# Reordered setup of a fused attention and ternary-MLP kernel, its 24 query transfers issued from three engines

## The reference

```
xn = layernorm(x)
h  = xn + cosformer_attn(rmsnorm(xn) * n1w)        # 16 heads of 16, relu(q), relu(k), cos/sin weights,
                                                    # cumulative sums over the 2048 positions
attention part:  h + gelu((rmsnorm(h) * n2w) @ W1 + b1) @ W2 + b2
ternary part:    r = relu(xn @ (tern(W_fc) * s_fc).T + gate * (xn @ V.T @ F.T @ U.T))
                 (r * r) @ (tern(W_proj) * s_proj).T
out = x + attention part + ternary part
```

## Time and profile before

| | us |
|---|---|
| median of three runs | 618.21 |
| the profiled execution: its time | 617.8 |
| the profiled execution: its span | 616.0 |
| PE busy | 586.7 (95%) |
| DVE busy | 409.2 (66%) |
| ACT busy | 364.4 (59%) |
| POOL busy | 221.4 (36%) |
| PE's first instruction of body(0) starts at | 40.14 |

### The profile page before, as it was taken

The page is one execution under the profiler, slowest core; times in us unless marked ns, Lnnn a source line. Parts: engine busy times, 40 slices in busy tenths (PEclk is TensorE's granted clock), DMA queues, the critical chain, the costliest instruction groups (busy, mean ns, idle before and its releaser), DMA issues.

```text
span 616.0 us, 14491 instructions
## 1 busy us (share of the span) xinstructions
PE 586.7 (95%) x5122; PEld 519.4 (84%) x5122; DVE 409.2 (66%) x776; ACT 364.4 (59%) x654; POOL 221.4 (36%) x251
## 2 busy tenths in 40 slices
PE   7768999999999999999999999999999999999996
PEld 6557888989898898988889898988989888898885
DVE  7899784686647865586746866478655867457532
ACT  6485674557646575557645576465754576455642
POOL 7035413372143612435143721436124351336220
PEclk9879999999999999999999999999999999999999
DMA  7871016400462006600163004610066001620001
GB/s 217 244 186 36 18 48 127 104 1 19 104 103 68 17 0 139 133 0 17 34 140 99 0 17 102 107 64 17 0 139 133 0 17 34 140 65 1 3 0 36
DMA packets 27994, 42.03 MB, mean 68 GB/s; under 512 B 9008, under 2 KB 19904, under 8 KB 27968
## 3 DMA queue, kind: packets, MB, share of 16 engines
q1 hardware_dynamic: 26528, 39.59, 27.7%
q10 hardware_dynamic: 1440, 2.10, 1.3%
HBM read 12.31 MB, written 4.19 MB: 27 GB/s over the span
## 4 chain that ended last, share of the span: by engine, by line
PE 84%; DVE 7%; ACT 4%; issue 2%; ACTq 1%; DMA 1%; DVEq 0%; SPq 0%
PE accum L1241 23%; PE dense L1406 9%; PE dense L1226 8%; PE shared L1264 5%; PE ctx_ps L1289 5%; PE dense L1411 5%; PE dense L1276 4%; PE dense L1134 4%; PE shared L1379 3%; PE shared L1148 3%; PE dense L1138 2%; PE dense L1231 2%; PE ctx_ps L1300 2%; PE upd_ps L1314 2%; PE shared L1358 1%
## 5 line engine op out<-in xcount | busy, mean ns | idle before, releaser
L977 DVE TENSOR_TENSOR wide_lo<-wide,wide_hi 128x512 fp32r<-128x512 f32 x128 | 94.7, 740 | 118.5 <-ACT wide_hi L695 100.1
L985 DVE TENSOR_TENSOR weighted<-shared,cst 128x512 f32<-128x512 f32 x128 | 82.8, 683 | 16.5 <-PE shared L1264 16.5
L692 ACT ACTIVATE wide<-dense,b 128x512 f32<-128x512 f32 x64 | 44.0, 688 | 83.1 <-PE dense L1411 82.7
L1241 PE MATMUL accum<-w_hi,wide_hi 128*128 128x256 f32 x256 | 72.6, 284 | 2.2 <-DVE wide_lo L977 2.2
L534 POOL TENSOR_TENSOR state<-state,added 128x544 f32<-128x544 f32 x32 | 43.8, 1369 | 80.7 <-DVE added L1007 80.4
L1241 PE MATMUL accum<-w_lo,wide_hi 128*128 128x256 f32 x256 | 71.8, 280 | 0.0
L1241 PE MATMUL accum<-w_hi,wide_lo 128*128 128x256 f32 x256 | 71.7, 280 | 0.0
L1241 PE MATMUL accum<-prT,wide_hi 128*128 128x256 f32 x256 | 66.1, 287 | 1.2 <-DVE wide_lo L977 1.2
L500 POOL TENSOR_TENSOR arena<-arena,tab 128x256 f32<-128x256 f32 x64 | 49.5, 802 | 43.7 <-DMA q_stack<-arena 43.7
L1241 PE MATMUL accum<-prT,wide_lo 128*128 128x256 f32 x256 | 64.7, 281 | 0.0
L682 ACT ACTIVATE wide<-dense,scales 128x512 f32<-128x512 f32 x64 | 43.9, 686 | 31.2 <-PE dense L1231 31.2
(11 more groups left out here) (176 smaller groups left out, 1490.5 us busy)
## 6 DMA issues: line engine op xcount, KB each, us to landing
k_stack<-weighted SPq DMA_DIRECT2D x96, 128.0 KB, 2.7
q_stack<-arena SPq DMA_DIRECT2D x184, 64.0 KB, 2.3
xin<-L_attn_x SPq DMA_DIRECT2D x16, 256.0 KB, 2.8
out<-late SPq DMA_DIRECT2D x16, 256.0 KB, 2.2
tab<-trig SPq DMA_DIRECT2D x8, 258.0 KB, 2.7
arena<-L_ffn_w_fc SPq DMA_DIRECT2D x1, 1024.0 KB, 7.4
late<-L_ffn_w_proj SPq DMA_DIRECT2D x1, 1024.0 KB, 7.4
late<-L_attn_mlp_w ACTq DMA_DIRECT2D x1, 1024.0 KB, 5.4
```

The costliest lines, as they stand in the source:

```text
L692: act.activation(wide[:, m % 2, :], dense[m % 2][:, :], ACT.Gelu_apprx_tanh, bias=b1[:, m:m + 1]).then_inc(dense_free, 1)
L977: dve.tensor_tensor(wide_lo[:, n % 2, :], wide[:, n % 2, :], wide_hi[:, n % 2, :].bitcast(F32), ALU.subtract).then_inc(lo_done, 1)
L985: dve.tensor_tensor(weighted[:, g, :].rearrange("p (a n) -> p a n", a=4), shared[g % 2][:, :].rearrange("p (a n) -> p a n", a=4), mask.rea ...
L1241: mm = pe.matmul(accum[k // 2][:, (k % 2) * E:(k % 2 + 1) * E], a[:, n % 2, tok], w[:, n % HB, :], start=(first and i == 0 and k % 2 == 0) ...
```

## The change

It touches only the setup and tile 0. The parts are:

1. `qkv_w` is scaled straight into its rounded part; the remainder is made in two instalments, first for q and k, then, behind the split of x, for v. `out_w` is split right after that and no longer near the end of setup.
2. ACT makes the rounded part of q (two copies); DVE makes only the remainders.
3. The q_hi transfers: g = 0, 1 are issued by POOL; g = 3 by ACT in two pairs, one ahead of and one behind the last two `fcT` reads; g = 2 by ACT behind the `gT` reads and the load of the second half of `W1`. SP keeps q_lo.
4. `u4` is made by one instruction for four. The remainder of `gT` comes ahead of the second step of `W_proj`; the v rows come behind it.
5. PE gets 8 more matmuls whose result is not used, behind the `u4` transposes.
6. `W2` is loaded in halves: ACT loads the first into `res`, SP the second into `xs`, once the first half of `W1` has been used. One quarter of it is split in each round.
7. In tile 0, `ffn_up(1)` comes ahead of the first scores on PE, `trig_v(0)` behind `ffn_block(1)` on ACT, and POOL's x + b2 waits for the second `split` of round 0.

```diff
+KEEP = 8
@@ (SP)
-                for g in range(2 if isinstance(t, int) and t == 0 else 4):
-                    for slot in (0, 2):
-                        stack_q(sp, g, slot, 0, q_hi_stacked[g // 2])
+                if not isinstance(t, int) or t:
+                    for g in range(4):
+                        for slot in (0, 2):
+                            stack_q(sp, g, slot, 0, q_hi_stacked[g // 2])
...
+            sp.wait_ge(w1_lo_done, 1)
+            sp.dma_start(raw_w2[1], mlp_w2[4 * P:8 * P, :].rearrange("(k p) n -> p k n", p=P)).then_inc(in_w2b, 16)
             load_next_x(0)
@@ (POOL)
             keep_msq(0)
+            pool.wait_ge(q_parts_done, 2 * KE)
+            pool.wait_ge(stack_zero, 3)
+            for g in range(2):
+                for slot in (0, 2):
+                    stack_q(pool, g, slot, 0, q_hi_by_pool)
...
                         pool.wait_ge(w1_lo_done, KE)
+                        pool.wait_ge(lo_done, 2)
                         for g in range(2):
                             x_plus_b2(0, g)
@@ (ACT)
             for i in range(1, 2 * KE):
                 relu_block(0, i)
+            act.wait_ge(qkv_split, 3 * KE)
+            for m in range(KE):
+                act.wait_ge(dense_free, KE + m + 1)
+                act.activation(q_parts[:, 0, m, :].bitcast(F32R), qT[:, m, :], ACT.Copy).then_inc(q_hi_made, 1)
             act.wait_ge(in_pr, 16)
...
-            for g in range(2, 4):
-                for slot in (0, 2):
-                    stack_q(act, g, slot, 0, q_hi_stacked[g // 2])
...
+            read_fc(0)
+            act.wait_ge(q_parts_done, 2 * KE)
+            stack_q(act, 3, 0, 0, q_hi_stacked[1])
+            read_fc(1)
+            stack_q(act, 3, 2, 0, q_hi_stacked[1])
...
             act.dma_start(raw_w1[1], mlp_w1[P:2 * P, :]).then_inc(in_w1[1], 16)
-
+            stack_q(act, 2, 0, 0, q_hi_stacked[1])
+            stack_q(act, 2, 2, 0, q_hi_stacked[1])
+            w1_hi_half(0)
             read(SET_SC, pr_scale_row[:, :], ctx_ps[:, 0:E])
-            w1_hi_half(0)
...
-            act.dma_start(raw_w2, mlp_w2.rearrange("(k p) n -> p k n", p=P)).then_inc(in_w2, 16)
+            act.dma_start(raw_w2[0], mlp_w2[0:4 * P, :].rearrange("(k p) n -> p k n", p=P)).then_inc(in_w2, 16)
...
-                            act.wait_ge(w1_lo_done, 1)
+                            act.wait_ge(w2_split, 4)
@@ (DVE)
+            def q_low_parts():
+                for m in range(KE):
+                    dve.wait_ge(q_hi_made, m + 1)
+                    dve.tensor_tensor(q_parts[:, 1, m, :].bitcast(F32R), qT[:, m, :], q_parts[:, 0, m, :],
+                                      ALU.subtract).then_inc(q_parts_done, 2)
...
-            split_weight(raw_qkv, in_qkv, wqkv_hi, wqkv_lo, qkv_split, n1w)
+            dve.wait_ge(in_qkv, 16)
+            for k in range(KE):
+                dve.tensor_scalar(wqkv_hi[:, k, :], raw_qkv[:, k, :], n1w[:, k:k + 1], None, ALU.mult).then_inc(qkv_split, 1)
...
+            qkv_lo(slice(0, 2 * E), KE)
...
             x_lo(0)
+            qkv_lo(slice(2 * E, 3 * E), 2 * KE)
...
+            split_weight(raw_wo, in_wo, wo_hi, wo_lo, wo_split)
...
-                    q_parts_split(0)
+                    q_low_parts()
...
             n = pr_ternary(0, n)
+            for g in range(2):
+                dve.wait_ge(read_out, SET_G + g + 1)
+                part = gT[32:64, g * TOK:(g + 1) * TOK]
+                dve.tensor_tensor(part, dense[g][32:64, :], part.bitcast(F32), ALU.subtract).then_inc(g_lo_done, 1)
+            n = pr_ternary(1, n)
+            z_lo(0)
...
+            w1_lo_half(0)
             dve.wait_ge(wo_split, 2)
             layernorm(0)
-            for k in range(KE):
-                w1_lo_half(k)
+            w1_lo_half(1)
...
-                    if setting_up:
-                        w2_quarter(2, 0)
                     weigh(j, 3)
-                    if setting_up:
-                        w2_quarter(3, 1)
-                    elif isinstance(t, int) and t == 0 and j >= 2:
-                        w2_quarter(j - 2, j)
+                    if isinstance(t, int) and t == 0:
+                        w2_quarter((j + 2) % 4, j)
@@ (PE)
-            pe.wait_ge(qkv_split, KE + 2)
+            pe.wait_ge(qkv_split, 2 * KE)
             make_kq(0, 0)
             make_kq(0, 1)
+            pe.wait_ge(qkv_split, 3 * KE)
...
-            pe.wait_ge(set_mem, 6)
+            for _ in range(KEEP):
+                pe.matmul(accum[0][:, 0:P], ones[:, :], ones[:, :], start=True, stop=True)
...
+                if isinstance(t, int) and t == 0:
+                    ffn_up(1)
                 scores(0, 0)
                 scores(0, 1)
-                ffn_up(1)
+                if not isinstance(t, int) or t:
+                    ffn_up(1)
```

More of the change, by code:

```diff
@@ L167, in program @@
         raw_pr = raw_late.rearrange("p (m n) -> p m n", m=KE)
-        raw_w2 = raw_late.rearrange("p (k n) -> p k n", k=HB)
+        raw_w2 = [t_[:, :, :] for t_ in (res, xs)]
         raw_w1 = [t_[:, :, :].rearrange("p b n -> p (b n)") for t_ in (xs, xb)]
@@ L358, in stack_q, with wait_q_hi @@
                                 q_parts[row:row + 16, part, :, :]).then_inc(done, 16)
+        def wait_q_hi(eng, t, i):
+            if i == 1:
+                eng.wait_ge(q_hi_stacked[1], (t + 1) * N_Q_HI * 16)
+            elif isinstance(t, int) and t == 0:
+                eng.wait_ge(q_hi_by_pool, N_Q_HI * 16)
+            else:
+                eng.wait_ge(q_hi_stacked[0], t * N_Q_HI * 16)
         block = ctx.enter_context(nc.Block())
@@ L709, in body @@
                 act.wait_ge(q_lo_stacked, (t + 1) * N_Q_LO * 16)
-                trig_v(0)
+                first = isinstance(t, int) and t == 0
+                if not first:
+                    trig_v(0)
                 ffn_block(0)
@@ L717, in body @@
                 ffn_block(1)
+                if first:
+                    trig_v(0)
                 def read_context(j):
@@ L808, in x_lo, with split_weight @@
                     x_lo_half(t, m)
-            def split_weight(src, load, hi, lo, done, scale=None):
-                steps = 0
+            def split_weight(src, load, hi, lo, done):
                 dve.wait_ge(load, 16)
-                if scale is not None:
-                    for k in range(KE):
-                        dve.tensor_scalar(src[:, k, :], src[:, k, :], scale[:, k:k + 1], None, ALU.mult).then_inc(done, 1)
-                        steps += 1
-                    dve.wait_ge(done, steps)
                 dve.tensor_copy(hi[:, :, :], src).then_inc(done, 1)
-                dve.wait_ge(done, steps + 1)
+                dve.wait_ge(done, 1)
                 dve.tensor_tensor(lo[:, :, :], src, hi[:, :, :].bitcast(F32), ALU.subtract).then_inc(done, 1)
@@ L878, in _, with qkv_lo @@
             dve.wait_ge(in_n1, 16)
-            split_weight(raw_qkv, in_qkv, wqkv_hi, wqkv_lo, qkv_split, n1w)
+            dve.wait_ge(in_qkv, 16)
+            for k in range(KE):
+                dve.tensor_scalar(wqkv_hi[:, k, :], raw_qkv[:, k, :], n1w[:, k:k + 1], None, ALU.mult).then_inc(qkv_split, 1)
+            def qkv_lo(cols, steps):
+                dve.wait_ge(qkv_split, steps)
+                for k in range(KE):
+                    dve.scalar_tensor_tensor(wqkv_lo[:, k, cols], raw_qkv[:, k, cols], n1w[:, k:k + 1],
+                                             wqkv_hi[:, k, cols].bitcast(F32), ALU.mult, ALU.subtract).then_inc(qkv_split, 1)
+            qkv_lo(slice(0, 2 * E), KE)
             dve.wait_ge(in_fb, 32)
@@ L958, in _ @@
             v_rows(0, 1)
-            n = pr_ternary(1, n)
-            z_lo(0)
-            for g in range(2):
-                dve.wait_ge(read_out, SET_G + g + 1)
-                part = gT[32:64, g * TOK:(g + 1) * TOK]
-                dve.tensor_tensor(part, dense[g][32:64, :], part.bitcast(F32), ALU.subtract).then_inc(g_lo_done, 1)
-            split_weight(raw_wo, in_wo, wo_hi, wo_lo, wo_split)
+            w1_lo_half(0)
             dve.wait_ge(wo_split, 2)
             layernorm(0)
-            for k in range(KE):
-                w1_lo_half(k)
+            w1_lo_half(1)
             dve.wait_ge(read_out, SET_SC + 1)
@@ L1019, in body @@
                 for j in range(NB):
-                    setting_up = isinstance(t, int) and t == 0 and j == 0
                     if j:
```

27 lines of the change are left out of this document (15 added, 12 removed).

## The result

The changed kernel takes 616.0 us in the median of six runs (614.96 to 616.49); the kernel before took 618.67 us in six runs. The ratio is 0.9955, with a 95% interval of 0.9941 to 0.9968: faster by 2.7 us. The forecast was 614.2 us in a range of 612.8 to 618.2. The direction is right, and the gain is two thirds of the 4.0 us forecast.

What follows compares the result with a forecast made beforehand. Setup was taken as bound by DVE, then ACT's issuing, then ACT's reads, with a second loss in body(0). Gains of 2.5 us at the start and 1.5 in body(0) gave 618.2 - 4.0 = 614.2 us, range 612.8 to 618.2.

Steps and rivals of the forecast that it cites:

- What bounds the kernel: Setup: DVE up to about 25 us, ACT's issuing up to 31.65, then ACT's reads; a second loss in body(0).
- Parts 1 and 2: Early setup: `zw` at 12.1, q parts complete at 23.6, last ternary step ending at 26.2, z copied at about 23.7.
- Part 3: Setup transfers: ACT's eight issues take 6.5 us in separate blocks, its reads come sooner, and POOL's transfers stay hidden.
- POOL's term: Setup: POOL's eight issues at 1.3 us each, bounds 0.59 and 1.74, hidden at either bound.
- The slower rival: Setup: POOL's transfers come late beside busy DVE and first scores wait; 626.7 us, or 621 at 2.6 an issue; chance 0.14.
- Parts 4 and 5: Late setup: unused matmuls cost up to 3.4 us and may restore the clock; body(0) starts between 37.1 and 38.5.
- Parts 6 and 7: body(0): round 0 drops from 7.41 to 5.95 us, 1.05 of it from one `W2` quarter; together 1.5 us.
- The step that failed: Round 1 of body(0): the added `W2` quarter fits DVE's 1.1 us idle time, costs nothing; step stays near 7.35.
- my signs of being wrong: Late POOL transfers, a POOL issue over 1.75 us, clock 0.50 beyond 34 us, third `across` moving under 3, changes behind it.
- it comes back elsewhere: Setup's end and body(0): `trig_q` and x + b2 slow DVE, the quarter delays statistics; 3 of 4 us gone, 617.5; chance 0.14.
- the smaller gain: Setup: clock stays low or ACT's issues get dearer, so only body(0) gains, 1 to 2 us: 616.7; chance 0.20.
- the likeliest case: Whole kernel: the forecast itself, 4.0 us gained, 614.2 us, by itself 612.9 to 615.6; chance 0.52.

Runs made afterwards that it cites:

- e11: The changed kernel with GpSimd's eight query transfers issued by ScalarE, two more at each of its four places: 620.9 us.
- e8: The changed kernel without the eight unused matmuls behind the `u4` transposes: 616.69 us.
- e4: The changed kernel with the `W2` quarters placed as before: two in round 0, none in round 1, one each in rounds 2 and 3: 616.63 us.
- e12: The changed kernel with statistics and moments of the next x behind round 2's products instead of round 1's: 614.06 us.
- e7: The changed kernel with all 16 transfers of the rounded q issued by GpSimd and none by ScalarE: 615.04 us.
- e1: The changed kernel with the eight query transfers of groups 0 and 1 issued by SP instead of GpSimd: 617.5 us.
- e9: The changed kernel with `W2` quarters and next-x statistics spread differently over tile 0's rounds, and GpSimd issuing all 16 rounded-q transfers: 615.95 us.
- e2: The changed kernel with eight more unused matmuls on PE in round 2 of body(0), ahead of `across`: 615.69 us.

## Why the prediction was right, and where it was short

**What bounds the kernel** was right: VectorE, then ACT's issues, then ACT's reads. e11 confirms the middle one by its price.

**Parts 1 and 2.** `zw` started at 12.30 (said: 12.1), the q parts were complete at 23.7 (23.6), the last ternary step ended at 26.4 (26.2), z was copied at 23.6 (23.7). All within 0.2 us.

**Part 3.** The start at 37.03 is just ahead of 37.1 to 38.5, and the same setup gave 36.6 to 37.7 in other profiles; the 2.5 us taken were 3.1. ACT's eight issues took 5.5 us and not 6.5; why they were cheaper than the 0.815 us each of the block before is not shown. POOL's term was missed the other way: 1.3 us each taken, within bounds of 0.59 and 1.74, and 0.56 measured, below the lower bound. It was hidden, so it changed nothing. The slower rival, transfers that starve beside VectorE, did not happen: VectorE was busy for 3.83 of the 4 us from 24 to 28 and the transfers went out at 0.48 us in the median. The figure of about 3100 ns that the Trainium skill ("SBUF — State Buffer", "SBUF: two separate sides") gives for a transfer beside a VectorE copy did not carry over. The figure is for one `tensor_copy`; here no instruction of VectorE's beside the eight issues was longer than 0.75 us, and none was a plain copy, so the runs do not test the rule itself. The transfers took 4.0 us to land, a little less than SP's 4.5 and ACT's 4.6 in the same profile.

**Parts 4 and 5.** The unused matmuls took 3.62 us at the clock of 0.50, a little over the bound of 3.4. The clock was back at 0.96 from 34 to 36 us, for the last transposes; in e8, without them, it was 0.50 there. That is worth 0.33 us of the start by e8's rows, not the 1.4 us between the forecast's two starts (37.1 and 38.5).

**Parts 6 and 7.** Round 0 went from 7.41 to 5.89, as forecast at 5.95, but not for the quarter of `W2` that I counted 1.05 us for: with both quarters in the round the step is still 5.96 (e4). The contention with x + b2, which I named second, accounts for all of it by e4's rows, so the number came out right in part by luck. `trig_q` did not run before the first scores (40.36) as I had said, but from 38.40 to 42.78. The first `across` came 7.09 us behind the start and not 6.7: 0.3 lost.

**The step that failed** is "DVE idled 1.1 us there before, so it costs nothing and the step stays near 7.35", and with it "nothing behind round 1 changes". The round-1 step became 8.32. The quarter did fit into VectorE's idle time, nearly: the statistics began 4.22 us behind the second `across` instead of 4.02. But that idle time had kept them off POOL's `trig_q`, and now they took 3.29 us instead of 2.60. The two make the 0.89 by which the stall grew. The lower clock behind it costs another 1.4 us: 7.42 for 6.02. Two of my signs of being wrong came true by this: the fourth `across` moved by 2.0 us where the third had moved by 3.4, and the clock was at 0.51 from 58 to 60 us.

The sum by the profiled executions: 3.11 at the start, less 0.33 to the first `across`, 1.52 in round 0, less 0.89 in round 1, less 1.40 in round 2, makes 2.01 us at the fourth `across` (67.76 to 65.75) and 2.2 at the end of the span. The time outside the span grew from 1.8 to 2.15 us, which gives 1.85; the profiled executions differ by 1.8. The medians differ by 2.7, as the profiled execution of the kernel before is 0.9 us below its median over six runs. Of the rivals, "it comes back elsewhere" named the right place (the statistics of round 1) and both causes (the quarter, and contention between POOL and VectorE), at a wrong size, and without the clock. The total of 616.0 lies in the range that was stated because that case and the smaller gain had been taken in; it lies above the 612.9 to 615.6 of the likeliest case.

## What to carry to other kernels

A DMA issue is cheap only on an engine that nobody waits for: the same eight issues delayed nothing visible on GpSimd, cost 1 to 2.3 us on SP and 4.9 us on ScalarE, and the way to see it is the idle time that the profile puts down to "issue". Idle time is not always free to fill: the 1.1 us that VectorE had in round 1 kept its statistics apart from GpSimd's work. When work is moved on either of the two, look up what the other then does in the new place: a two-input addition of four columns took 0.69 us beside GpSimd, and 0.16 without it. And a stall that grows from 1.4 to 2.3 us is not priced by its 0.9 us: in six profiles of eight TensorE came out of it at the lower clock, for another 1.4 us; moving the statistics one round on (e12) left a stall of 1.49 us without the fall and gave 614.1 us, better than both kernels. Last, profile a kernel more than once before reading a difference of less than 1 us out of its setup.

## What the runs showed that I had not expected

A 64 KB transfer was issued by GpSimd in 0.53 to 0.56 us (8 in 4.47, 16 in 8.43), beside a VectorE that hardly paused: it was busy for 8.76 of the 9 us from 24 to 33 in e7.

The time outside the span was 1.80 us on average for the kernel before and 1.79 for e1, 2.09 to 2.16 for all kernels with eight GpSimd transfers, and 2.49 and 2.47 for those with sixteen (e7, e9). It looks like 0.35 us for each eight; but e11, which has none, shows 2.06, so GpSimd's transfers are not shown to be the cause, and it stays open.

What decides whether the clock falls behind a stall of 2.3 us (it did in six profiles of eight) also stays open; the e2 matmuls did not settle it.
